# Edge counting in groups of six nodes and two rows of 128 edges, with source one-hots in two batches for a block

## The reference, cut to what matters

```python
h = x @ W_in.T + b_in
for i in range(3):
    src_feat = h[edge_src]
    agg = scatter_logsumexp(src_feat, edge_dst, N)      # log of the sum over incoming edges of exp(h[src])
    hc = concatenate([h, agg], axis=-1)
    h_new = relu(layer_norm(hc @ W_l[i].T + b_l[i], gamma_l[i], beta_l[i]))
    h = 0.5 * h + 0.5 * h_new
...
h1 = silu(concatenate([node_feats[src], edge_sh, edge_radial]) @ W1 + b1)   # per edge
messages = silu(h1 @ W2 + b2) @ W3 + b3
aggregated = segment_sum(messages, dst)
...
```

## Time and profile before

| | |
|---|---|
| median of 3 runs | 3612.53 us (3607.04 to 3618.94) |
| profiled execution, its own time | 3614.43 us |
| its span in the profile | 3612.2 us |
| busy in the span: PE, PEld | 2970.1 us (82%), 2102.1 us (58%) |
| busy in the span: DVE, ACT, POOL | 1628.9 us (45%), 1389.0 us (38%), 1591.1 us (44%) |
| mean granted TensorE clock | 0.837 of 2.4 GHz |

### The profile page before, as it was taken

How to read it: one execution, slowest core, us unless ns; L and a number is a source line. 1 busy time by engine, 2 the same in 40 slices (tenths; PEclk the granted TensorE clock), 3 DMA queues, 4 the chain that set the end, 5 groups by cost and what they waited for, 6 DMA issues and landing times.

```text
span 3612.2 us, 59613 instructions
## 1 busy us (share of the span) xinstructions
PE 2970.1 (82%) x17152; PEld 2102.1 (58%) x17152; DVE 1628.9 (45%) x3492; ACT 1389.0 (38%) x2083; POOL 1591.1 (44%) x1667
## 2 busy tenths in 40 slices
PE   3799999985986985788888898888888888888855
PEld 2577777765986985444554555445455454555455
DVE  7999999985015017322222222222222222222227
ACT  2788888872001001233333333333333333333312
POOL 4000000000000000777777777777777777777642
PEclk7899999997996995788878778888878888787756
DMA  3122222234973961466666666666666666666510
GB/s 115 72 124 107 124 107 124 107 148 190 395 320 139 395 264 57 118 165 164 163 163 166 164 161 167 168 164 162 166 163 166 164 166 164 164 164 165 140 35 18
DMA packets 352485, 576.87 MB, mean 160 GB/s; under 512 B 41884, under 2 KB 248862, under 8 KB 333384
## 3 DMA queue, kind: packets, MB, share of 16 engines
q1 hardware_dynamic: 299480, 467.64, 38.6%
q0 software_dynamic: 52976, 108.89, 14.0%
HBM read 388.48 MB, written 187.88 MB: 160 GB/s over the span
## 4 chain that ended last, share of the span: by engine, by line
POOL 31%; PE 24%; issue 18%; DVE 17%; DMA 7%; DVEq 2%; ACT 1%; POOLq 1%; ACTq 0%; SPq 0%
POOL arena L541 29%; PE ps L665 11%; DVE arena L1330 9%; DMA arena<-p_tab,m_idx 6%; PE ps L742 4%; PE ps L584 3%; PE ps L751 2%; PE ps L739 2%; PE ps L572 1%; DVEq L1330 1%; POOL ends L509 1%; PE ps L759 1%; DVE arena L1317 1%; DVE ybuf L1202 1%; DVE ends L1023 1%
## 5 line engine op out<-in xcount | busy, mean ns | idle before, releaser
L541 POOL DMA_INDIRECT arena<-p_tab,m_idx x1568 | 1486.5, 948 | 1864.6 <-issue 1832.3
L1406 DVE TENSOR_TENSOR_SCAN arena<-arena,ps 128x512 f32<-128x512 f32 x392 | 501.6, 1280 | 1036.5 <-ACT ps L922 937.8
L742 PEld LDWEIGHTS ps<-ident,arena 128*128 128x128 f32 x3136 | 488.0, 237 | 623.2 <-DMA arena<-p_tab,m_idx 463.9
L742 PE MATMUL ps<-ident,arena 128*128 128x128 f32 x3136 | 579.6, 342 | 278.6 <-DMA arena<-p_tab,m_idx 278.6
L917 ACT ACTIVATE arena<-ps 128x512 f32<-128x512 f32 x392 | 234.0, 597 | 1030.1 <-PE ps L742 1017.2
L665 PE MATMUL ps<-arena 128*128 128x192 bf16 (+1 forms) x5635 | 505.6, 248 | 66.7 <-DVE arena L1275 65.8
L751 PE MATMUL ps<-arena,weights 128*128 128x512 f32 x784 | 540.5, 782 | 0.0
L665 PEld LDWEIGHTS ps<-arena 128*128 128x128 f16 x5635 | 481.8, 98 | 81.1 <-issue 66.1
L1330 DVE TENSOR_SCALAR arena<-iota_w,arena 128x392 bf16<-128x392 f16 x2156 | 519.5, 314 | 0.0
L682 PE MATMUL ps<-arena 128*128 128x392 bf16 x2352 | 452.1, 336 | 70.9 <-DVE arena L1330 70.6
L739 PE MATMUL ps<-arena,weights 17*128 17x512 f32 x784 | 487.7, 704 | 0.0
(11 more groups left out here) (187 smaller groups left out, 1675.8 us busy)
## 6 DMA issues: line engine op xcount, KB each, us to landing
arena<-count_d SPq DMA_DIRECT2D x66, 1568.0 KB, 8.2
arena<-keep_d SPq DMA_DIRECT2D x392, 256.0 KB, 4.5
scan_rows<-arena SPq DMA_DIRECT2D x392, 256.0 KB
count_d<-arena SPq DMA_DIRECT2D x49, 1568.0 KB, 5.2
wide<-count_d SPq DMA_DIRECT2D x32, 1568.0 KB, 8.4
arena<-p_tab,m_idx POOLq DMA_INDIRECT x1568
arena<-attr_in SPq DMA_DIRECT2D x392, 34.0 KB
p_tab<-wide SPq DMA_DIRECT2D x7, 448.0 KB, 3.0
```

The source lines that it names most:

```text
L541: pool.indirect_dma_start(m_rows[:, k, t, :], None, p_tab, bass.IndirectOffsetOnAxis(ap=m_idx[:, k, t:t + 1].bitcast(U32), axis=0))\
L742: last = pe.matmul(x[:, t * P:(t + 1) * P], m_rows[:, k, t, :], ident[:, :], start=False, stop=(t == TB - 1), skip_group_check=True)
L1406: dve.tensor_tensor_scan(m_scan[:, k % SCAN_RING, :], m_mask[:, k, :], m_term[k % TERM_RING], before, ALU.mult, ALU.add).then_inc(e1.scan_ ...
```

## The change

Groups have WD = 6 nodes and WT = 2 rows of 128 edges. A block of 128 has WB = 22 groups, 20 of six nodes and at its end two of four (LAST_WD). Groups of five blocks (110) lie on the lanes, WG = 10 columns, NW = 1,100 groups with those of one block that isn't there. The first edge of a group is rounded down to a multiple of GE = 8. Each group takes two matmuls of 294 columns. ScalarE copies 11 pairs of groups a block (ten of 588 columns, the last of 392), and makes the second key one-hot of groups 3, 7, 11 and 15 (ACT_HOTS = 4); VectorE makes the other 40. The source one-hots of a block come in two batches of 11 groups (22 x 128 = 2,816 columns), the second ahead of the one-hots of group 6, the first of the next block ahead of those of group 17. The first layer's sums for block j are spread behind the groups 3 to 21 of block j + 1. In the setup: ten columns to search (five on VectorE), ten fetches of rows, 20 fetches of edge rows, ten rounds of keys, and eight more small instructions that work out each lane's block and first node; `iota_s` has 22 x 128 numbers and lies over `stage`. Padded edges have destination 1 << 20. Five semaphores that only balanced increments became one (`alone`).

```diff
-WD = 8
-NW = NPAD // WD
-WB = P // WD
-WT = 3
+WD = 6
+WB = -(-P // WD)
+LAST_WD = (P - (WB - 2) * WD) // 2
+BLOCKS = 5
+WQ = BLOCKS * WB
+WG = -(-J // BLOCKS)
+NW = WQ * WG
+WT = 2
 WE = WT * P
-GE = 32
+GE = 8
-DVE_SEARCHES = 4
+DVE_SEARCHES = 5
 WSLOTS = 4
-QUAD = WSLOTS * WT
-DVE_HOTS = QUAD - 1
-QUADS = WB // WSLOTS
+PAIRS = WB // 2
+ACT_HOTS = 4
+BATCH = WB // 2
+HOT_COLS = BATCH * WT
+DVE_HOTS = WB * WT - ACT_HOTS
+NO_DST = 1 << 20
+SUMS_FROM = 3
...
+                def count_window(j, k, r):
+
+                    w = WB * j + k
+                    slot, b = (WB * r + k) % WSLOTS, k // BATCH
+                    if k % BATCH == 0:
+                        pe.wait_ge(src_hot_ready, 2 * j + b + 1)
+                    if k % 2 == 0:
+                        pe.wait_ge(bank_free, w // 2 + 1 if isinstance(w, int) else PAIRS * j + k // 2 + 1)
+                    pe.wait_ge(hot_ready, DVE_HOTS * j + WT * (k + 1) - min((k + 1) // 4, ACT_HOTS))
+                    if k % 4 == 3 and k // 4 < ACT_HOTS:
+                        pe.wait_ge(act_hot_ready, ACT_HOTS * j + k // 4 + 1)
+                    for i in range(WT):
+                        last = pe.matmul(ps[:, 4 + slot, 0:WCOLS], hot_b[b][:, :, (k % BATCH) * WT + i], hot_a[:, slot, i, :],
+                                         start=(i == 0), stop=(i == WT - 1))
+                    last.then_inc(win_counted, 1)
...
-                        for q in range(QUADS):
-                            count_windows(j + 1, q)
-                            if q == 0:
+                        for k in range(WB):
+                            count_window(j + 1, k, 1 - r)
+                            if k == SUMS_FROM:
                                 first_sums_ready(j)
-                            if q < QUADS - 1:
-                                block_sums(j, r, first_parts, q * J // (QUADS - 1), (q + 1) * J // (QUADS - 1))
+                            if k >= SUMS_FROM:
+                                n = k - SUMS_FROM
+                                block_sums(j, r, first_parts, n * J // (WB - SUMS_FROM), (n + 1) * J // (WB - SUMS_FROM))
...
-                    for m in range(WB // 2):
-                        two = 4 + 2 * (m % 2)
+                    for m in range(PAIRS):
+                        two, wd = 4 + 2 * ((PAIRS * r + m) % 2), WD if m < PAIRS - 1 else LAST_WD
                         act.wait_ge(win_counted, WB * j + 2 * (m + 1) + WSLOTS)
...
-                        if m % 2 == 1 and not (last and m == WB // 2 - 1):
-                            one_hot(QUADS * j + m // 2 + 1)
+                        after = 2 * m + WSLOTS + 1
+                        if after % 4 == 3 and after // 4 < ACT_HOTS:
+                            one_hot(j, after, r)
+                        if m == PAIRS - 1 and not last:
+                            one_hot(j + 1, 3, 1 - r)
...
+                def source_hots(j, b):
+
+                    keys = keyT_b[:, bass.ds(WB * j + BATCH * b, BATCH), :].rearrange("p w i -> p (w i)")
+                    dve.tensor_tensor(hot_b[b], iota_s[:, :, :], keys.unsqueeze(1).to_broadcast([P, P, HOT_COLS]),
                                       ALU.is_equal).then_inc(src_hot_ready, 1)
...
+                def one_hots(j, r):
+
+                    for k in range(WB):
+                        w, slot = WB * j + k, (WB * r + k) % WSLOTS
+                        if k % 2 == 0:
+                            dve.wait_ge(win_counted, w + 2)
+                        if k == BATCH // 2 + 1:
+                            source_hots(j, 1)
+                        if k == BATCH + BATCH // 2 + 1:
+                            source_hots(j + 1, 0)
+                        for t in range(WT - (k % 4 == 3 and k // 4 < ACT_HOTS)):
+                            dve.tensor_scalar(hot_a[:, slot, t, :], iota_w[:, :], keyT_a[:, t, bass.ds(w, 1)], None, ALU.is_equal)\
+                                .then_inc(hot_ready, 1)
```

More of the change, by code:

```diff
@@ L175, in build @@
         iota_i = carve(WIN_AT + 2 * WG * P, WCOLS).bitcast(I32)
-        hi_at = WIN_AT + 2 * WG * P + WCOLS
-        key_hi = [carve(hi_at + n * WE, WE, WQ).bitcast(I32).rearrange("p (i e) -> p i e", i=WT) for n in range(2)]
+        key_hi = [carve(4 * ET + n * WE, WE, WQ).bitcast(I32).rearrange("p (i e) -> p i e", i=WT) for n in range(2)]
         firsts = carve(16416, ET).bitcast(I32)
@@ L317, in build @@
         gate_in, gate_done, x_summed = (sem(n) for n in ("gate_in", "gate_done", "x_summed"))
-        alone = {e: sem("alone_" + e) for e in ("sp", "act", "pe", "pool", "dve")}
+        alone = sem("alone")
         block = ctx.enter_context(nc.Block())
@@ L401, in by_counts @@
                     sp.wait_ge(block_used, l * J + RING)
-                    sp.sem_inc(alone["sp"], 1)
+                    sp.sem_inc(alone, 1)
                     with sp.Fori(0, BODIES) as i:
@@ L501, in gather @@
                     pool.wait_ge(e.idx_ready, SLOTS * c + k + 1)
-                    pool.sem_inc(alone["pool"], 1)
+                    pool.sem_inc(alone, 1)
                     for t in range(TB):
@@ L569, in turn @@
                 pe.wait_ge(node_copied, n + 1)
-                pe.sem_inc(alone["pe"], 1)
+                pe.sem_inc(alone, 1)
                 for t in range(GT):
@@ L668, in block_sums @@
                         last.then_inc(block_used, 1)
[L670 to L684 removed]
+                def count_window(j, k, r):
[12 more added lines that the diff above has]
+                    last.then_inc(win_counted, 1)
                 def first_sums_ready(j):
[L687 removed]
+                    pe.wait_ge(block_part, PAIRS * (j + 1))
                     pe.wait_ge(sums_read, j + 1)
@@ L890, in one_hot @@
                     act.wait_ge(square_ready, n + 1)
-                    act.activation(hot_a[:, WSLOTS - 1, WT - 1, :], squares, ACT.Relu, scale=-1.0, bias=ones[:, 0:1])\
+                    act.activation(hot_a[:, (WB * r + k) % WSLOTS, WT - 1, :], squares, ACT.Relu, scale=-1.0, bias=ones[:, 0:1])\
                         .then_inc(act_hot_ready, 1)
                 exponential(0, first_parts)
-                one_hot(0)
+                one_hot(0, 3, 0)
                 with act.Fori(0, J // 2) as i:
@@ L1042, in node_phase @@
                     dve.wait_ge(squares_summed, 2 * (square[0] + NG))
-                dve.sem_inc(alone["dve"], 1)
+                dve.sem_inc(alone, 1)
             dve.sem_inc(node_used, 2)
@@ L1098, in _ @@
             dve.sem_inc(h_ready, 1)
+            link(dve.tensor_copy(iota_s[:, :, :], iota_i[:, 0:P].unsqueeze(2).to_broadcast([P, P, HOT_COLS])))
             dve.wait_ge(edges_loaded, 2 * DMA)
@@ L1471 @@
     src[:N_EDGES] = a["src"]
-    dst = np.full(EPAD, NPAD, i32)
+    dst = np.full(EPAD, NO_DST, i32)
     dst[:N_EDGES] = a["dst"]
```

107 lines of the change are left out of this document (46 added, 61 removed).

## The result

| | before | after |
|---|---|---|
| median, runs taken side by side | 3613.56 us (4 runs) | 3664.11 us (4 runs, 3655.91 to 3692.39) |
| ratio | | 1.0155 (95% interval 1.0094 to 1.0215) |
| profiled execution, its span | 3614.43, 3612.2 us | 3656.25, 3654.3 us |
| counting starts, ends | 110.7, 793.5 us | 118.8, 853.2 us |
| a block of counting, mean | 13.94 us | 15.02 us |

The change is slower by 50.6 us in the medians and by 42 in the two profiled executions. The prediction said 3635 and slower: the sign and the range held, but the loss is more than twice the one forecast (22 us).

A forecast was written before the change was run, and what follows sets the result against it. VectorE bounded counting at 13.94 us a block; ScalarE would next, 13.6 plus 0.6 of stalls, 14.2. 3614.4 + 13 (49 blocks) + 9 (setup) = 3636.5, the median 1.9 lower: 3635 us, range 3602 to 3684.

The forecast's parts named there:

- VectorE is relieved of some 2 us and stops being the bound: Counting: VectorE's block falls by 2.3 to 11.6 us, with one-hots 0.206 apart and batches of 1.54.
- Rival 3: Counting: one-hots of 294 columns run at a slower rate, 0.28 us each, giving 3668 us; chance 0.13.
- TensorE: Counting: TensorE's block falls from 12.2 to 9.9 us, leaving only latency; it idles on one-hots twice a block.
- rival 2: Counting: the clock falls as TensorE is less busy, +0.7 to +0.9 us a block, 3675 us; chance 0.15.
- ScalarE's own work: Counting: eleven fills and four one-hot pairs take ScalarE from 13.1 to 13.6 us a block, the new bound.
- rival 1: Counting: ScalarE runs at its floor of 13.6 us a block with no stall, 3606 us; chance 0.19.
- rival 4: Counting: ScalarE's gaps are hidden or fills cheaper, VectorE sets the pace, block 12.4 us, 3547 us; chance 0.10.
- The stalls: Counting: ScalarE waits 0.25 us at each of two source batches and 0.1 at the block's end, 0.6 a block.
- C + 3.0: Counting, batch behind group 16's one-hots: pair 8 is counted 3.0 us after C, when pair 6 is counted; stall 0.25.
- Rival 5: Counting: a group over two rows of edges sends everything by edges, many times slower; no chance worth a number.
- Setup: Before counting: longer by 9 us (5 to 14), including 4 for fetched tile rows and 1.3 for keys.
- only shifted: Everything from 866 us on, after counting, keeps its length and merely comes later.

The follow-up runs named there:

- e2: Changed kernel with its two source batches split into four of 1,536 and 1,280 columns, ahead of groups 4, 9, 15 and 20: block 15.02 us, ratio 1.0169.
- e5: Changed kernel with ScalarE's four one-hots moved to groups 3, 9, 15 and 21: block 15.08 us, ratio 1.0185.
- e9: Changed kernel with both source batches ahead of VectorE's waits for counted groups, one moved from group 17 to 16: block 14.77 us, ratio 1.0146.
- e10: Changed kernel with the reduce ahead of group 4 of the next block but one and source batches ahead of VectorE's waits: block 13.73 us, ratio 1.0009.
- e1: Changed kernel with VectorE's reduce of a block's sums moved ahead of group 4 of the next block but one: block 14.37 us, ratio 1.0119.
- e12: Changed kernel with late reduce, source batches ahead of VectorE's waits, and two ScalarE one-hots (groups 3 and 15): block 12.54 us, ratio 0.9856.
- e7: Changed kernel with late reduce and three ScalarE one-hots instead of four (groups 3, 11 and 19): block 14.38 us, ratio 1.0089.
- e6: Changed kernel with late reduce and ScalarE's four one-hots at groups 3, 9, 15 and 21: block 14.38 us, ratio 1.0082.
- e3: Changed kernel with late reduce and the two source batches split into four: block 14.33 us, ratio 1.0057.
- e8: Changed kernel with late reduce and two ScalarE one-hots instead of four (groups 3 and 15), whole batches: block 13.59 us, ratio 0.9970.

## Why the prediction was right and where it failed

- **VectorE is relieved of some 2 us and stops being the bound: right.** It is 81% busy in counting. One-hots are 0.295 us long and stand 0.206 apart in short runs (7 in 1.53 us) and 0.22 in long ones (11 from 403.99 to 406.42); a batch is followed 1.54 later. Rival 3, slower one-hots at 0.28, is out.
- **TensorE: right.** A group matmul every 0.125, a sum every 0.086. The granted clock of a stretch of 100 us in counting is 1.00, of the whole stage 0.99, so rival 2 is out for this kernel, though TensorE was busy 78%. It was not groundless: in e2, e5 and e9 some blocks had half clock for a stretch and were 0.5 to 1.5 us longer. TensorE idles on one-hots not twice a block, as forecast, but four times: twice on VectorE's (1.38 or 0.98, and 1.06 us) and twice on ScalarE's (0.47 us each).
- **ScalarE's own work: right to 0.3.** The fills, by form:

```profile
L890 ACT ACTIVATE arena<-ps 128x588 f16<-128x588 f32 x490 | 321.2, 655 | 130.4 <-PE ps L692 109.0 <-ACT arena L890 21.1
...
L890 ACT ACTIVATE arena<-ps 128x392 f16<-128x392 f32 x48 | 23.9, 497 | 13.0 <-PE ps L692 13.0
```

  655 and 497 ns against 0.66 and 0.50. Only the gap from a fill to its one-hot was 0.22 instead of 0.29 in three cases of four: 13.3 against 13.6. That is a gain of 0.3 which the block never saw. Of rival 1 (floor, no stalls) and rival 4 the runs say that the gaps remain (0.18 in every run) and that the floor is reached by no order tried with four one-hots on ScalarE: 13.73 in e10 is the nearest.
- **The stalls: right in kind and in place, wrong in size; this is the step that failed.** Predicted 0.25 ahead of fill 8, 0.25 ahead of fill 3, 0.1 at the block's end, 0.6 in all; measured 0.50, 0.50, 0.51 on average, and 0.18 ahead of fills 9 and 10, 1.7 in all. For fill 8 the chain "C + 3.0" was exact (one-hot 413.30, fill 416.31). But ScalarE was due after 3.73 instead of 3.85 by the shorter gap, and C came 1.2 instead of 1.1 behind: 4.23 - 3.73 = 0.50. A stall is a difference of two sums near 4 us; an error of 0.1 in each doubled it. At the block's end the sums, reduce and one-hots took 2.5 and 2.1 us in turn (402.96 to 405.47, 418.18 to 420.30) instead of 2.0, the extra 0.4 being the loop's turn, which the prediction did not have, and ScalarE's own part was 1.8 instead of 1.9. And the three are not independent, as it had them: the batch ahead of group 6 starts at 406.42, right behind the 11 one-hots which the reduce had held up, so that fill 3 was late from the block's end rather than from pair 0. e1 shows both: 0.65 us a block by the reduce's place alone.
- **Block 15.02 instead of 14.2**, 0.2 above the top that I gave it; x 49 that is the 39 us between +13 and +52. That the time stayed in the range is partly luck. With the top of its own block (14.8, +42) and the setup's +9 the sum ends at 3663, just under the 3664 measured; the range went on to 3684 for rivals 2 and 3, which the rows rule out.
- **Two slips in the sums**, without weight: the steps given for fill 8 add up to 3.83, not 3.85, and rival 1's -17 + 9 gives 3605, not 3606.
- **Rival 5: out.** The counting matmuls (L692) are in the trace, so the way by counts was taken.
- **Setup: right.** +8.1 against +9; the wait for the tile rows +4.2 against +4, keys 15.1 us against 14.7 before, so +0.4 instead of +1.3.
- **The rest "only shifted": not in this pair of executions**; 17 us came back in phases with a higher granted clock, by chance. Without it the profiled time would have been some 3673. How much of it is in the medians no trace shows.
- **The place of the fault in method.** The three engines' sums (11.6, 9.9, 13.6) were good to 3%, and the time did not follow them, for the order in the queues decides. e10 against the kernel after is the proof: same instructions in another order, 1.3 us of 15.0. Adding up the stalls one by one, each measured from a different engine's free state, gave a third of the truth; the measured round (last fill to the next first fill 2.3 on average, from there 4.06 to fill 3, 6.78 to fill 8, 1.87 to the last fill) is 15.0, and its second link, reduce, 11 one-hots, batch, group 6, fill 3, crosses all three engines.

What stays open: how much of e12's gain is the 294-column groups and how much the order. The kernel before with its batches ahead of the waits wasn't tried; its VectorE had no gap to win there, so I expect nothing of it. Nor is it shown why e7 and e6, e1 and e3 end within 0.05 of 14.35; a common chain of batch, group 6 and reduce is likely, and was only argued. How much of e9's gain is the wait and how much the batch's earlier place among the one-hots was not separated.

## What to carry to other kernels

When three engines pass work round a ring with few slots, shares of busy time and sums by engine tell only the floor: follow one whole round in the order of each queue and add the links. Look in each queue for long work that stands behind a wait which it doesn't need, and move it ahead of that wait, the longest first; that took no work away and, for the reduce and the batches together, was worth 1.3 of 15.0 us here. Shift work from the engine that sums highest only after that: the same shift of two one-hots gave 0.78 us with the batches behind the waits (14.37 to 13.59) and 1.19 with them ahead (13.73 to 12.54).

## What the runs showed of the hardware

- The node phases between the sums take 66 to 67 us or 74 to 76, with no value between, in the profiled executions of all these kernels: 67.0 and 74.4 in the kernel before, 66.6 and 66.4 after, 75.3 and 74.4 in e1, 67.1 and 66.3 in e3, 75.7 and 66.3 in e8 (from TensorE's last sum to its next). The short ones have a mean granted clock of 0.67 to 0.69, the long ones 0.52 to 0.54, and TensorE is busy 19 or 20 us in the short ones and 31 or 32 in the long ones with the same matmuls.
- The setup of the changed kernels ends at 118 to 119 us or at 133, and at 141 to 143 on the chip of e9 to e12. Between the kernel after and e1 the 14 us lie in the matmuls of the input product: 14 of them take 1.77 us in one and 3.25 in the other, though the record of the granted clock reads 1.00 in both from 30 to 60 us. So a matmul's length can double where this record shows nothing.

```profile
46.72 1.77 PE L594 MATMUL ps<-weights,stageT 64*128 64x64 f32 x14
```
```profile
48.82 3.25 PE L595 MATMUL ps<-weights,stageT 64*128 64x64 f32 x14
```

- So single times of one kernel can differ by 30 us (8 + 8 + 14) from these two alone, more than half of what the change did, and a difference of that size is better read from the stage it is in.
- In e2, e5 and e9 half clock came in short stretches in counting, each less than 2.5 us after TensorE had idled 0.97 to 1.40 us at a block's end. The kernel after idles 1.38 and 0.98 us there too and has no such stretch in its blocks, so the idle time alone does not decide it.
- A loop's turn shows on VectorE as 0.30 us of "issue" in the kernel after, where it follows a wait, as 0.17 in e1 and 0.22 in e10, and as nothing in e12, where VectorE never waits.
- Another chip ran the same kernel before at 4209 instead of 3613 us. The instructions of counting had the same lengths there; the 1,568 gathers of the message stage took 2513 us from first to last in e9 instead of the 1963 of the kernels before and after. That is 550 us, most of the 596 by which the kernel before differs. An absolute time of such a kernel holds for its chip; the ratios and the blocks are what can be compared.
- An estimate from the Trainium skill ("VectorE: DVE Perf Modes", the errata-adjusted cycle table) gives the one-hot of 294 columns 0.137 us. The runs have it at 0.206 to 0.22 from start to start, so they disagree, as the earlier trace rows did for 392 columns. From 0.231 and 0.206 for the two sizes one gets 0.025 us for 98 columns; by that estimate some 0.13 us of a one-hot is fixed.
